# Local attention layers of a fused model: scores and outputs in separate banks, one projection block per sequence, inverse norms on ScalarE, rotated halves added by GpSimd

## The reference

```python
def attn_layer(x, Wqkv, qs, ksc, Wo):          # 16 heads of 64, window 32
    q, k, v = split(x @ Wqkv); q, k = l2norm(q) * qs, l2norm(k) * ksc
    q = q * cos * scale + rotate_half(q) * sin * scale
    k = k * cos / scale + rotate_half(k) * sin / scale
    out = local_attention(q, k, v)              # a query sees its block of 32 keys and the one before
    return out @ Wo

def ffn_layer(x, g, bln, W1, b1, W2, b2):       # inner size 341
    xn = (x - mu) / sqrt(var + 1e-5) * g + bln
    a, gate = split(xn @ W1 + b1)
    return a * gelu(gate) @ W2 + b2
```

## Time and profile before

| | |
|---|---|
| median of 3 runs | 2530.72 us (2529.07 to 2532.38) |
| the profiled execution | 2530.31 us, span 2528.5 us, 98074 instructions, mean granted clock 0.991 |
| PE busy | 2403.8 us (95%) |
| DVE, ACT, POOL busy | 1996.5 (79%), 1882.5 (74%), 1765.6 us (70%) |
| the chain that ended last | PE 82%, DVE 9%, issue 5%, POOL 2%, ACT 1% |

### The profile page before, as it was taken

The page is one execution under the profiler, slowest core; times in us unless marked ns, Lnnn a source line. Parts: engine busy times, 40 slices in busy tenths (PEclk is TensorE's granted clock), DMA queues, the critical chain, the costliest instruction groups (busy, mean ns, idle before and its releaser), DMA issues.

```text
span 2528.5 us, 98074 instructions
## 1 busy us (share of the span) xinstructions
PE 2403.8 (95%) x36438; PEld 1705.2 (67%) x36442; DVE 1996.5 (79%) x4388; ACT 1882.5 (74%) x6630; POOL 1765.6 (70%) x1605
## 2 busy tenths in 40 slices
PE   7999888879999999999999999999999999799999
PEld 6888555546666666666666666666667666477874
DVE  5555699978888888888888888888888888655644
ACT  4777799868888888888888888888888888533323
POOL 2888887488888888888888888888888888222200
PEclk9999999999999999999999999999999999999999
DMA  4111211021112111211112111211121111100000
GB/s 123 15 15 15 52 14 14 10 85 36 33 33 66 38 37 33 59 42 42 33 41 59 42 33 34 64 38 40 33 54 47 41 33 33 34 1 1 1 1 17
DMA packets 177876, 91.06 MB, mean 36 GB/s; under 512 B 40974, under 2 KB 174328, under 8 KB 177408
## 3 DMA queue, kind: packets, MB, share of 16 engines
q1 hardware_dynamic: 168574, 80.42, 11.8%
q0 software_dynamic: 8192, 4.21, 1.5%
q10 hardware_dynamic: 642, 0.15, 0.0%
HBM read 30.57 MB, written 3.76 MB: 14 GB/s over the span
## 4 chain that ended last, share of the span: by engine, by line
PE 82%; DVE 9%; issue 5%; POOL 2%; ACT 1%; SPq 0%; DMA 0%; DVEq 0%; POOLq 0%; ACTq 0%
PE bank L1197 13%; PE bank L1214 9%; PE scores L1249 7%; PE bank L1260 7%; PE bank L1204 6%; PE scores L1231 6%; PE bank L1186 3%; PE bank L1292 3%; PE bank L1310 2%; PE bank L1301 2%; PE bank L639 2%; PE scores L1225 2%; DVE rg_prod L1011 2%; PE scores L671 2%; PE bank L1934 1%
## 5 line engine op out<-in xcount | busy, mean ns | idle before, releaser
L1636 POOL TENSOR_TENSOR rs<-ssc,neg_half 128x8 f32<-128x8 f32 x384 | 643.4, 1675 | 38.9 <-DVE ssc L1456 38.9
L1626 POOL TENSOR_TENSOR t_pair<-qn_pair,tabs 128x512 f32<-128x512 f32 x384 | 488.6, 1272 | 12.2 <-DVE qn_pair L1444 11.6
L1564 ACT ACTIVATE pr<-scores,negmax 128x64 f32<-128x64 f32 x1536 | 460.3, 311 | 48.8 <-DVE negmax L1464 23.8
L1616 POOL TENSOR_TENSOR pr<-pr,rec 128x256 f32<-128x256 f32 x384 | 235.1, 612 | 282.8 <-DVE rec L1436 282.8
L1197 PE MATMUL bank<-wqk,xs 128*128 128x512 f32 x768 | 402.5, 606 | 12.4 <-DVE qn_pair L1444 11.3
L1564 ACT ACTIVATION_READ_ACCUMULATOR pr<-scores,negmax 128x1 f32 x1536 | 311.3, 203 | 0.0
L1083 POOL DMA_INDIRECT rg_win<-rg_images,share_down x256 | 256.4, 1002 | 71.2 <-issue 54.9
L1452 DVE TENSOR_REDUCE ss<-sq 128x8 f32<-128x512 f32 x384 | 260.8, 679 | 33.4 <-ACT sq L1587 32.4
L1444 DVE TENSOR_TENSOR qn_pair<-bank,rs 128x512 f32<-128x512 f32 x384 | 257.1, 670 | 27.1 <-POOL rs L1636 27.0
L1555 ACT COPY vt<-bank 128x256 f32<-128x256 f32 x361 | 135.1, 374 | 188.4 <-issue 187.3
L1214 PE MATMUL bank<-oT,wo 128*128 128x128 f32 x1536 | 266.2, 296 | 0.0
(11 more groups left out here) (313 smaller groups left out, 5494.4 us busy)
## 6 DMA issues: line engine op xcount, KB each, us to landing
rg_prod<-vt SPq DMA_DIRECT2D x1536, 32.0 KB, 1.9
wqk<-in_L_ffn_Wqkv SPq DMA_DIRECT2D x20, 256.0 KB
rg_win<-rg_images,share_down POOLq DMA_INDIRECT x256
wv<-in_L_ffn_Wqkv SPq DMA_DIRECT2D x20, 128.0 KB
wo<-in_L_ffn_Wo SPq DMA_DIRECT2D x20, 128.0 KB, 2.6
w<-in_L_ffn_W SPq DMA_DIRECT2D x6, 341.0 KB
rg_images<-rg_prod SPq DMA_DIRECT2D x1, 1625.0 KB, 9.3
ZT<-in_x SPq DMA_DIRECT2D x4, 256.0 KB, 3.9
```

The lines of the kernel that those rows point to most:

```text
L1564: ex = act.activation(pr[t % 2][:, h * BAND:(h + 1) * BAND], sl_ps[:, h // 2, h % 2 * BAND:(h % 2 + 1) * BAND], ACT.Exp, bias=negmax[t % 2 ...
L1626: pool.tensor_tensor(t2[t % 2][:, :].rearrange("p (i h f e) -> p i h f e", i=2, h=GH, f=2), qn[t % 2][:, :].rearrange("p (i h f e) -> p i ...
L1636: pool.tensor_tensor(rs[t % 2][:, :], ssc[t % 2][:, :], neg_half[:, 0:8], ALU.pow)\
```

## The change

Seven things change, all in the local layers.

1. PSUM: scores keep two banks of their own. Values, probabilities' transposes, outputs and the projection share the two banks of a new tensor `moves` (banks 4 and 5). S no longer waits for the outputs' copy, and the maximum no longer for AT. In exchange V and TP wait for the copy of the last outputs, TP and AT for the sum into `ZT` of a block that is projected in the same slot, and AT for V's copy of its own slot.
2. The projection is one block of eight products per sequence (`project(b)`), in slots that `LATER` gives: slots 15, 19, 23 and 25 for the first four sequences, and so on every sixteen.
3. Inverse norms: on ScalarE as exp(-0.5 ln x), two small instructions in turn with a semaphore `logged` between, instead of the power on GpSimd. In the slot after the Gelu's GpSimd still does the power (`inverse_norms`).
4. The sum of the rotated halves goes from VectorE to GpSimd (`turned`).
5. The copy of V goes from ScalarE to VectorE in every slot, with four `vt` buffers instead of three.
6. The lags are shorter (AT at 7 instead of 8, S at 5 instead of 6), VectorE's head sums are a slot later, and the orders within the slots are new. The first chunk of the feed-forward starts at slot 28 instead of 25, and TAIL is 396 instead of 393.
7. ScalarE loads its table by name at the start and after each Gelu, instead of by an unread Exp.

```diff
-L_QKV, L_ROPE, L_COS, L_SUM, L_TURN, L_SCORE, L_V, L_MOVE, L_EXP, L_PROB, L_PROJ = 1, 2, 3, 4, 5, 6, 5, 6, 7, 8, 9
-FFN_FIRST, FFN_EVERY = TICKS // NCH + L_PROJ, TICKS // NCH
+L_QKV, L_ROPE, L_COS, L_SUM, L_TURN, L_V, L_SCORE, L_EXP, L_PROB, L_OUT, L_PROJ = 1, 2, 3, 3, 4, 4, 5, 6, 7, 8, 10
+FFN_FIRST, FFN_EVERY = 28, TICKS // NCH
-LATER = {0: (1, 2), 1: (2, 1), 8: (10, 0), 9: (10, 1)}
+LATER = (2, 2, 2, 0)
...
-        bank = [ctx.enter_context(nc.psum_tensor(f"bank{i}", [P, 512], F32)) for i in range(6)]
+        bank = [ctx.enter_context(nc.psum_tensor(f"bank{i}", [P, 512], F32)) for i in range(4)]
+        moves = ctx.enter_context(nc.psum_tensor("moves", [P, 2, 512], F32))
+        bank += [moves[:, i, :] for i in range(2)]
...
-        vl_ps, pTl_ps, yl_ps = bank[4][:, 0:GV], bank[4][:, GV:GV + GB], bank[5][:, 0:P]
-        sl_ps, ol_ps = scores[:, :, 0:P], scores[:, :, P:2 * P]
+        vl_ps, pTl_ps, yl_ps = bank[4][:, 0:GV], bank[5][:, 0:GB], bank[5][:, GB + P:GB + 2 * P]
+        sl_ps, ol_ps = scores[:, :, 0:P], moves[:, :, GB:GB + P]
...
+        def projected_at(u):
+
+            for b in range(LOCAL // GROUPS):
+                if GROUPS * b + GROUPS - 1 + L_PROJ + LATER[b % GROUPS] == u:
+                    return b
+            return None
+
+        PROJECTED = list(itertools.accumulate(0 if projected_at(u) is None else 1 for u in range(SLOTS)))
+
+        def until(t):
+
+            return TICKS + min(max(t, 0), LOCAL)
...
             def turn_probs(t, u):
                 pe.wait_ge(a.p_scaled, TICKS + t + 1)
                 pe.wait_ge(a.pT_moved, TICKS + t)
-                pe.wait_ge(a.v_moved, TICKS + min(u - 1 - L_V, LOCAL - 1) + 1)
+                pe.wait_ge(a.oT_moved, until(u - L_PROB))
+                pe.wait_ge(a.added, B + PROJECTED[u])
...
+            def project(b, u):
+                l = b // B
+                pe.wait_ge(a.oT_moved, until(max(GROUPS * (b + 1), u - L_PROB)))
+                pe.wait_ge(a.pT_moved, until(u - L_PROB))
+                pe.wait_ge(s.wo_loaded, 32 + 64 * l)
+                pe.wait_ge(a.added, B + b)
+                for c in range(2 * GROUPS):
+                    mm = pe.matmul(yl_ps, wo[:, c, :], oT[b % 2][:, c * P:(c + 1) * P],
+                                   start=(c == 0), stop=(c == 2 * GROUPS - 1))
+                mm.then_inc(a.y_ready, GROUPS)
...
-            def score(t, u):
+            def score(t):
                 pe.wait_ge(a.qkT_moved, TICKS + t + 1)
                 pe.wait_ge(a.exp_ready, TICKS + t)
-                if live(u - 1 - L_PROB):
-                    pe.wait_ge(a.oT_moved, TICKS + u - L_PROB)
...
                 pe.wait_ge(a.pT_moved, TICKS + t + 1)
                 pe.wait_ge(a.v_spread[t % 2], 64 * (t // 2 + 1))
                 pe.wait_ge(a.oT_moved, TICKS + t)
-                if live(u - L_EXP):
-                    pe.wait_ge(a.exp_ready, TICKS + u - L_EXP + 1)
+                pe.wait_ge(a.v_moved, until(u - L_V + 1))
+                pe.wait_ge(a.added, B + PROJECTED[u])
...
-            def values(t):
+            def values(t, u):
                 l, b, g = t // TICKS, t // GROUPS, t % GROUPS
                 pe.wait_ge(a.v_moved, TICKS + t)
-                pe.wait_ge(a.pT_moved, TICKS + max(t + L_V - L_PROB + 1, 0))
+                pe.wait_ge(a.oT_moved, until(u - L_PROB))
...
+            def inverse_root(t):
+                act.wait_ge(a.clamped, t + 1)
+                if t >= 2:
+                    act.wait_ge(a.normed, t - 1)
+                act.activation(rs[t % 2][:, :], ssc[t % 2][:, :], ACT.Ln).then_inc(a.logged, 1)
+                act.wait_ge(a.logged, LOGS[t])
+                act.activation(rs[t % 2][:, :], rs[t % 2][:, :], ACT.Exp, scale=-0.5).then_inc(a.rs_ready, 1)
+
+            act.preload_act_table_set("natural_log_exp_and_others")
...
+            def turned(t):
+                if live(t):
+                    pool.wait_ge(a.roped_c, t + 1)
+                    pool.wait_ge(a.roped_s, t + 1)
+                    if t >= 2:
+                        pool.wait_ge(a.qkT_ready, t - 1)
+                    pool.tensor_tensor(qr[t % 2][:, :], t1[t % 2][:, :], t2[t % 2][:, :], ALU.add)\
+                        .then_inc(a.qr_ready, 1)
...
+            def slot(u):
+                inverse_deviations(u)
+                sines(u - L_COS)
+                turned(u - L_SUM)
+                scaled(u - L_EXP)
+                if bursts(u):
+                    inverse_norms(u - L_QKV)
```

More of the change, by code:

```diff
@@ L1 @@
 from contextlib import ExitStack
+import itertools
 import numpy as np
@@ L558, in _ @@
                 if live(t):
-                    near, far = vt[t % 3], vx[t % 2]
+                    near, far = vt[t % GROUPS], vx[t % 2]
                     sp.wait_ge(a.v_moved, TICKS + t + 1)
@@ L1136, in ffn_bank @@
             return bank[LAST_BANKS[step]] if c == DEPTH * NCH - 1 else ffn_ps
[L1138 to L1144, removed]
+        def projected_at(u):
[6 more added lines that the diff above has]
+            return TICKS + min(max(t, 0), LOCAL)
         def bursts(u):
             return ffn_step(u)[1] == F_GELU
+        LOGS = list(itertools.accumulate(0 if bursts(t + L_QKV) else 1 for t in range(LOCAL)))
         def types_dve(dve, part):
@@ L1314, in pe_local, with feed_forward @@
             pe.wait_ge(s.wqkv_loaded, 16 * 10)
[L1315 to L1325 removed]
+            def feed_forward(u):
                 c, step = ffn_step(u)
@@ L1472, in pT_copy, with outputs @@
                     dve.tensor_copy(pT[t % 2][:, 0:GB], pTl_ps).then_inc(a.pT_moved, 1)
-            def slot(u):
-                t = u - L_PROJ
-                if live(t) and bursts(u - 1):
+            def outputs(t):
+                if live(t):
                     b, g = t // GROUPS, t % GROUPS
@@ L1600, in slot, with qkT_copy @@
                     ffn(c, step)
-                t = u - L_TURN
-                if live(t) and not bursts(u):
+            def qkT_copy(t):
+                if live(t):
                     act.wait_ge(a.qkT_ready, t + 1)
@@ L1605, in slot @@
                     act.copy(qkT[t % 2][:, :], turn_ps[:, :]).then_inc(a.qkT_moved, 1)
+            shifted(0)
+            def slot(u):
+                if not bursts(u - 1):
+                    outputs(u - L_OUT)
+                exponentials(u - L_EXP)
+                if (u + 1) % GROUPS == 0:
+                    shifted((u + 1) // GROUPS)
+                if live(u - L_ROPE) and not bursts(u - 1):
+                    inverse_root(u - L_ROPE)
+                pT_copy(u)
+                squares(u - L_QKV)
+                feed_forward(u)
+                if not bursts(u) and not bursts(u - 1):
+                    qkT_copy(u - L_TURN)
             for u in range(TAIL):
@@ L1610, in pool_local, with inverse_deviations, sines @@
         def pool_local(pool):
-            def slot(u):
-                t = u - L_EXP
-                if live(t):
-                    pool.wait_ge(a.rec_ready, TICKS + t + 1)
-                    p = pr[t % 2][:, 0:GB].rearrange("p (h k) -> p h k", h=GH)
-                    pool.tensor_tensor(p, p, over(rec[t % 2][:, :], [P, GH, BAND], 2), ALU.mult).then_inc(a.p_scaled, 1)
-                t = u - L_ROPE
+            def inverse_deviations(u):
+                c, step = ffn_step(u - 1)
+                if step == F_VAR:
+                    pool.wait_ge(s.lf_vareps, c + 1)
+                    if c:
+                        pool.wait_ge(s.lf_spread, c)
+                    pool.tensor_tensor(xr[:, :], xv[:, :], neg_half[:, 0:CH], ALU.pow).then_inc(s.lf_rstd, 1)
+            def sines(t):
                 if live(t):
```

202 lines of the change are left out of this document (86 added, 116 removed).

## The result

| | before | after |
|---|---|---|
| median, us | 2529.89 (2528.85 to 2532.38) | 2632.06 (2631.22 to 2633.46) |
| profiled execution, span us | 2528.5 | 2631.6 |
| ratio to before, 95% interval | | 1.0403 (1.0385 to 1.0421) |

Slower by 102 us, where 12 us faster was forecast; the time lies far outside the range. The first rows answer to the earlier trace rows: the timeline of PE at the first Q, at the Q of slots 28 and 380, and at the mean product of the last feed-forward chunk, which follows the last projection (start, us, engine, line, operation, tiles).

A forecast was written before the change was run, and what follows sets the result against it. PE was taken as the bound by order and load, with 66.9 us of work a cycle. Sum: 2530.3 + 2 (steady part) - 2 (start) - 12 (end) = 2518 us; own range 2508 to 2530, range for all 2492 to 2553.

The forecast's parts named there:

- v_spread keeps two slots from AT of t-2 to AT of t, never under 5.8, and the weight loads three; nothing: V's transfers and weight loads on SP's queue: claimed to keep enough room after the change, adding no wait.
- Steady part: The twenty-two feed-forward cycles: 2.3 us lost a cycle against 2.2 before, together +2 us.
- step 11 behind the Gelu: Slot after the Gelu: scores wait for exponentials behind Gelu and table loads, stall 0.8 plus restart 0.2 us.
- the short slots: Four slots a cycle with 3.12 us of PE work: ScalarE's chain and V's copy cost 0.5 us a cycle.
- step 3: Slot whose projection block stands first behind Q: block waits for the outputs' copy, 0.35 plus restart 0.2 us.
- step 6: The 3.56 us slot: GpSimd's slack carries the preceding short slots but for about 0.25 us here.
- Start: Fill slots before the first feed-forward cycle: 93 us against 94.9 before, gain 2, for three slots more.
- End: Last phase, from slot 380 on: only five of sixteen slots full, 48.8 us against 61.0, gain 12.
- Rival 1: Uneven slots not evened out, short ones cost 3.65 us from VectorE-GpSimd exclusion: cycle 70.65, 2549 us; chance 0.22.
- Rival 2: Free running: only the Gelu's loss is left, short slots cost 3.12 us: cycle 68.1, 2493 us; chance 0.22.
- Rival 3: No change: 0.6 to 0.8 us more a cycle in waits for the outputs' copy, 2531 to 2536 us; chance 0.14.
- rival 4: ScalarE's alternating Ln and Exp force two table loads of 1.28 us a slot, over 900 us more; chance 0.01.

The follow-up runs named there:

- experiment 1: Changed kernel with both feed-forward weight load points four ticks later (LOAD_UP, LOAD_DOWN = 21, 24 instead of 17, 20): 2559.86 us.
- Experiment 2: Kernel before with only both weight load points four ticks earlier (LOAD_UP, LOAD_DOWN = 13, 16 instead of 17, 20): 2608.92 us.
- experiment 5: On experiment 1, VectorE's three rotation-table products, once a layer, moved from a short slot to slot 35, which has a projection block: 2555.04 us.
- experiment 6: Kernel before with inverse norms on ScalarE as Ln and Exp, GpSimd's power only in the slot after the Gelu's: 2580.72 us.
- experiment 8: On experiment 1, the sum of the rotated halves moved back from GpSimd to VectorE, behind the norm product: 2622.86 us.
- experiment 9: On experiment 5, each chunk's second projection block one slot earlier, LATER = (2, 1, 2, 0) instead of (2, 2, 2, 0): 2545.83 us.
- experiment 4: On experiment 1, the first three projection blocks of a chunk moved into short slots, LATER = (1, 0, 1, 0) instead of (2, 2, 2, 0): 2605.15 us.

## Why the prediction was wrong

**The step that failed** is the sentence "v_spread keeps two slots from AT of t-2 to AT of t, never under 5.8, and the weight loads three; nothing". It counts the room that `v_spread` has between two AT, and takes for granted that SP comes to it in time. In the rows SP issues the spreads only when the load ahead of them has gone out (W1's has to land as well), and the change moves what the loads wait for by four slots against SP's ticks. So the price was not nothing: AT waited 6.3 and 4.2 us in each of five layers, and with the slow slots behind these waits that is 72 us by experiment 1. Experiment 2 shows the same price (+78) with nothing else changed.

**Steady part, +2 forecast, +105 measured.** The loads are 72 of it. The rest is +33: 15 in the regular cycle (0.68 each) and 18 in single slots. The slots of the cycle shown first, beside those that the pieces of the earlier trace rows give without waits:

| step | 7 | 8 | 9 | 10 | 11 | 12 | 13 | 14 | 15 | 0 | 1 | 2 | 3 | 4 | 5 | 6 |
|---|---|---|---|---|---|---|---|---|---|---|---|---|---|---|---|---|
| measured | 5.86 | 3.98 | 3.98 | 3.36 | 6.56 | 3.98 | 5.77 | 3.98 | 3.98 | 3.98 | 4.35 | 3.31 | 5.99 | 3.16 | 3.54 | 4.05 |
| no waits | 5.78 | 3.98 | 3.98 | 3.12 | 5.78 | 3.98 | 5.78 | 3.98 | 3.98 | 3.98 | 3.98 | 3.12 | 5.71 | 3.12 | 3.12 | 3.56 |

The product count and the 66.9 us were right, to 0.02 in seven slots. The waits were mostly of the forecast kind, but not of the forecast size: step 11 behind the Gelu loses 0.8 (1.0 forecast), the short slots 0.9 (0.5), step 3 0.3 (0.55), step 6 0.5 (0.25), and step 1 has 0.37 that I had not seen; together 2.9, not 2.3. In the cycle from 1276.9 us the timelines name them. The block of step 3 and V of step 1 start 0.05 and 0.10 behind the end of the outputs' copy; in step 11 the block starts as late behind that copy (0.27 late), and the mask product waits for the exponentials (0.4 late); TP waits 0.17 and 0.28 for GpSimd's scaling in steps 5 and 6.

**What I had no term for.** VectorE's tables once a layer fall into a short slot, now that V's copy is on VectorE: 2.4 us for AT (experiment 5). I costed the regular cycle only, and of the 103 us by which the steady part was off, 90 are in things that happen once a layer or rarer.

**Start, 93 forecast, 98.9 measured.** Fill slots are 3.70 for 3.65; the sum is 1.27 us and not the 1.15 that I took between two bounds, and it was the upper bound that held. Neither makes much: the larger part is that four fill slots have a block; three take 5.27 and one 4.94 where I had given all of them 3.65: 6.1 us, less 0.2 in the other slots.

**End, 12 gained forecast, 12 measured for the phase that the forecast meant.** From slot 380 to the end of the last P it is 49.0 us, 48.8 forecast. The mean product behind it then comes 5.5 us later, where it was 3.8 before, so that 10 of the 12 are left in the rows above.

**The rivals.** None was what happened. Rival 1 (2549, uneven slots) comes near the time without the load fault, 2560, but not by its mechanism: short slots take 3.2 to 3.5 and not 3.65. Rival 2 does not hold: its cycle was 68.1. Rival 3 had the regular cycle best: it put 0.6 to 0.8 more on it in waits for the outputs' copy, the cycle is 0.7 longer than before, and steps 1, 3 and 11 have 0.9 of such waits where the forecast had 0.55. But it had nothing for what happens once a layer. The table loads between Ln and Exp (rival 4) do not occur: the trace has two a Gelu and no others in the steady part.

**What is good of the change** can now be said by parts. ScalarE's norms, V's copy on VectorE and the sum on GpSimd need one another: the norms without the rest cost 50 us (experiment 6), the whole without the sum 63 (experiment 8). Together they still gain nothing over the old order, which has 69.15 us a cycle where they have 69.4 to 69.8. What the separate banks and the shorter lags do alone no run tests. Even the best version here, experiment 9, is 0.5% slower than the kernel before. What would take the last 16 us is open in part. In experiment 9 the cycle is 0.3 too long, step 7 takes 5.7 instead of 4.2 in the five cycles in which VectorE makes the tables, and step 11 takes 7.7 and 9.2 in the two in which it makes the type weights, the 9.2 with a stretch of granted clock 0.50. None of these was tried alone.

## What to carry to other kernels

When a change shifts one stage against another, list every queue that keeps a count of its own, weight loads above all, and ask for each what it waits for now and what is queued behind it; a load that waits too early stops all later transfers of its queue. Cost what happens once a layer as well as the regular cycle, and look at the list of slot lengths before any mean. Work put ahead of what another engine waits for is paid there (experiments 4 and 6). An engine's busy share does not tell whether relieving it helps: with 24 us a cycle taken from GpSimd and 4.5 us put on ScalarE, the cycle grew by 2.

## What the runs showed of the hardware

A long wait of PE costs more than its length. Windows of the changed kernel behind the wait of 6.33 us (us, busy PE, PEld, DVE, ACT, POOL, then the granted clock):

```profile
889.30:892.10 2.80, 2.80 (x9) 1.47 (x6) 0.00 (x0) 1.87 (x11) 0.00 (x0) 0.50 0.18 47
892.10:894.70 2.60, 2.60 (x67) 1.83 (x65) 1.34 (x4) 1.35 (x3) 1.24 (x2) 0.96 0.14 32
894.80:898.70 3.90, 3.90 (x73) 2.54 (x70) 2.90 (x8) 3.73 (x16) 2.09 (x3) 1.00 0.00 0
```

Behind the wait the clock stands at 0.50, the 1.2 GHz level, for the first 2.8 us: from Q's start to V's it is 1.87 us, where the earlier trace rows has 1.05 behind AT, and V's row is 1.06 long, which is 0.60 in the slot ahead of the wait. The slot behind the long one is 5.44 instead of 3.98, so this wait of 6.3 us cost 6.7 + 1.5 = 8.2. All ten such waits of the changed kernel (4.2 to 6.3 us) have a stretch of 0.50 behind them; in the ten slots behind them PE has no wait of over 0.15 us, the mean granted clock is 0.59 to 0.74, and they are 1.0 to 2.3 us longer than the same steps elsewhere. Behind the 20 waits of 2.6 us in experiment 4 it fell 11 times. Behind the wait of 0.94 us in the earlier trace rows, and in all 22 cycles of the kernel before, it stayed at 1.00.

The sum of two plain 128x512 tensors on GpSimd took 1.27 us, as long as the product with reversed halves (1.30); the product of two operands without a reversal in the earlier trace rows took 1.04. I have no run that says what makes the difference.
